# Order of every engine's work written by a list schedule at build time, in an attention and mixture-of-experts layer

## The chip, the cores and the metric

One core of one Trainium2 chip runs the whole kernel. The metric is the device time in microseconds of one execution. Below, PE is TensorE, DVE is VectorE, ACT is ScalarE, POOL is GpSimd and SP is the engine that issues the plain transfers.

## The reference

Eight sequences of 512 rows of 128 numbers go through one layer.

```
q, k, v = x @ Wq, x @ Wk, x @ Wv             # 16 heads of 8 numbers; q and k are rotated (rope)
attn = softmax(causal(q @ k.T / sqrt(8)))    # 512 x 512 per head
x1 = layernorm(x + (attn @ v) @ Wo)
shared = (silu(x1 @ sw1) * (x1 @ sw3)) @ sw2                 # every row, width 256
logits = x1 @ router_w.T + experts_bias; two best of 8 experts, softmax over the two
moe = sum over the two of weight * (silu(x1 @ w1[e]) * (x1 @ w3[e])) @ w2[e]
out = layernorm(x1 + moe + shared)
```

## The kernel before

The work is cut into small parts, each with a kind and a key. Sequence s is in the keys; so `values.2.1` is the part `values` of sequence 2 with its second group of four heads. For each sequence PE does `x_T` (x is transposed), `project` twice (q and k with their rotated copies), `v`, then bursts. A `burst` is the unit of the scores: it makes scores of one block of heads for the row maxima, which DVE takes from them (`max`), and, for the block three blocks earlier (`LEAD = 3`), the scores again with the maxima in them, of which ACT takes the exponential (`scores` on ACT) and on which POOL zeroes what the causal mask hides (`scores` on POOL). Four blocks of five bursts make a sequence, 40 units of scores. The maxima go through PE (`max_rows`), DVE and an SP transfer (`maxima`) into the stack of q and k that the second scores read; q and k themselves are split in three bf16 parts (`rope`, `rest`, `low`, on POOL and ACT, for the first sequence on DVE), stored (`store_parts`) and loaded back (`stack`). `values` multiplies the masked exponentials by v, for ten units each; `heads_T`, `out_T`, `out`, then on DVE `ln1_stats` and `ln1` (with a power on POOL between them) give x1. PE transposes it (`x1_T`) and computes the router's logits (`router`).

The expert part is made of steps: a shared step per 128 rows, and routed tiles of 128 rows sorted by expert. Groups of sequences are sorted together: `SORTED = [[0, 1], [2, 3], [4, 5], [6], [7]]`, which makes 23 tiles for a pair and 15 for one. For a group PE counts (`count`, `rank`), POOL writes the rows of x1 to their places in memory (`scatter`, eight per sequence), SP loads them in fours (`load_rows`) and loads the weights of each tile (`weight`, a ring of four). Per step: `T` (rows transposed), `gate` on PE, `tanh` on ACT, `glu` on DVE, `down` on PE. Results are stored (`store_rows`), gathered by POOL (`gather`), and finished by DVE (`combine`, `ln2_stats`, `ln2`).

Every engine runs its own fixed list and waits at semaphores when what it needs isn't there. What sets the lists is one table. A time in units of scores stands for each kind in `AT`; `LATER` moves a kind on one engine; each engine's list is all events sorted by that time:

```
        return [(kind, key) for _, _, kind, key in
                sorted((at + LATER.get((engine, kind), 0), n, kind, key) for at, n, kind, key in events if kind != "step")]
```

PSUM is shared by order too: the small results of PE take two banks in turn (`RING`), the projections, maxima scores and heads take two others in turn (`m_use`), so an engine's place in the list also decides which bank it waits for. Lines that the steps below touch: L665 `x_T`, L673 `project`, L679 `v`, L686 the scores of a burst, L719 `max_rows`, L732 `values`, L744 `heads_T`, L766 `x1_T`, L773 `router`, L826 `gate`, L838 `down`, all on PE; L903 `max`, L945 `ln1` and `ln2` on DVE, L1029 and L1037 `glu`; L548 the exponentials and L561 `rope` on ACT; L484 the masks, L496 `scatter`, L506 `gather`, L332 `rope` on POOL; L361 `store_parts`, L374 `stack`, L380 `maxima` on SP.

Of the kernel before, what the change touches and what calls it, by code (L numbers as in the profile page):

```python
# [27 lines left out]
SORTED = [[0, 1], [2, 3], [4, 5], [6], [7]]  # L28

AT = dict(values=2.39, v=9.96, rows1=12.08, maxima1=11.92, heads_T0=3.87, heads_T1=5.09, out_T=6.97, out=8.09,
          ln1_stats=8.24, ln1=9.29, x1_T=10.6, router=10.9, weights=11.33, load_residual=-9.49, load_x=-66.56,
          x_T=-58.7, project0=-56.05, project1=-57.45, rope=-52.94, rest=-50.5, low=-45.97, store_parts=-42.99,
          stack0=-39.65, stack1=-15.2, rows0=-8.24, maxima0=-8.23, count=12.23, rank=12.56, scatter=14.13,
          scatter_step=0.52, shared=11.71, shared_step=2.7, routed=28.08, margin=1.02, apart=1.0, T=-1.89, tanh=-0.0,
          glu=0.16, down=1.98, stored=4.65, weight_late=1.33, gather=6.58, gather_step=1.39, combine=1.9,
          lull_from=-4.81, lull_to=17.29, lull=1.0, routed_last_but_one=-0.14, routed_last=0.07, apart_last=1.0,
          gather_last=7.56, gather_step_last=1.43, combine_last=7.65)


LATER = {("act", "T"): 0.17, ("act", "ln1"): -0.41, ("act", "ln2"): 0.14, ("act", "out"): -0.33, ("act", "rest"): 2.75,
         ("act", "rope"): 2.16, ("act", "weights"): 0.16, ("act", "x_T"): -0.18, ("dve", "count"): -0.5,
         ("dve", "max"): 0.18, ("dve", "max_rows"): -0.5, ("dve", "rank"): 0.28, ("dve", "router"): -0.5,
         ("pool", "ln2"): -0.33, ("pool", "low"): -0.5, ("pool", "product"): 1.64, ("pool", "rest"): 0.55,
         ("pool", "rope"): -0.5, ("pool", "scores"): 0.76, ("pool", "shared_rows"): 0.44}


def build_block(nc, x, wq, wk, wqr, wkr, wv, wo, cos, sin, ident, mask, router, bias, experts, consts, out):
    B, S, D = x.shape  # L50
# [5 lines left out]
    T = S // P  # L56
# [115 lines left out]
    STEP = [key for _, key in steps]  # L172
    step_of = {key: i for i, key in enumerate(STEP)}

    def line(engine):
# [5 lines left out]
    RING = ("x_T", "v", "values", "max_rows", "out_T", "out", "x1_T", "router", "count", "rank", "T", "down")  # L181
# [31 lines left out]
    with ExitStack() as ctx:  # L213
# [437 lines left out]
        def _(pe):  # L651
# [37 lines left out]
            def burst(n, b):  # L689

                scored = n - LEAD
                if scored >= 0:
                    s, block = scored // BLOCKS, scored % BLOCKS
                    half = scored // 2
                    first = NU * 2 * scored + 2 * b
                    if scored % 2 == 0 and b == 0:
                        pe.wait_ge(max_in, (half + 1) * 48)
                    for pair in range(2):
                        if first + pair >= 2:
                            pe.wait_ge(exp_done, first + pair - 1)  # L700
                        for at_piece, (k, j, at) in enumerate(PAIR_UNITS[b]):
# [450 lines left out]
```

## Time and profile before

| | us |
|---|---|
| median of three runs | 780.66 (780.32 to 781.21) |
| the profiled execution, its own time | 776.18 |
| span in the profile | 774.1 |
| PE busy | 600.5 (78%) |
| DVE busy | 475.7 (61%) |
| ACT busy | 323.9 (42%) |
| POOL busy | 322.0 (42%) |

Busy time is the sum of an engine's instructions. The span less the busy time is what an engine waited, for other engines, for transfers, or for nothing that the profile can name ("issue"). The mean clock granted to PE over the span was 0.864 of full speed.

### The profile page before, as it was taken

How to read it: one execution, taken by the hardware profiler on the slowest of the kernel's cores; microseconds unless marked ns; L12 is line 12 of the kernel's file. 1: busy time of each engine (PE TensorE's matmuls, PEld its weight loads, DVE VectorE, ACT ScalarE, POOL GpSimd, SP SyncE). 2: the span in 40 equal slices, each digit the busy share in tenths (PEclk: the TensorE clock that was granted, in tenths of full speed). 3: DMA queues.
4: the chain of work that ended last, by engine and by line, in shares of the span. 5: the costliest groups of instructions: out<-in, count | busy, mean ns of one | idle time of the engine just before them, and what ended most of it. 6: DMA issues, size and time to landing. Idle time of an engine off the chain costs nothing.

```text
span 774.1 us, 14746 instructions
## 1 busy us (share of the span) xinstructions
PE 600.5 (78%) x4363; PEld 381.2 (49%) x4363; DVE 475.7 (61%) x1957; ACT 323.9 (42%) x771; POOL 322.0 (42%) x530
## 2 busy tenths in 40 slices
PE   3378988887878889888887998887898887786650
PEld 1123224424534565466544754655566665586640
DVE  3477747675537777776568877765578731644342
ACT  2016543563226455643364447524464455213320
POOL 4033431262275223424686326218447445442313
PEclk9567868978679999999899899979799999868985
DMA  3742220220224634622455345413575375435741
GB/s 92 214 143 87 63 91 2 76 83 8 70 89 141 185 93 130 180 93 86 153 163 149 94 151 157 127 47 122 159 217 169 93 210 165 133 102 158 203 111 54
DMA packets 80062, 94.08 MB, mean 122 GB/s; under 512 B 10224, under 2 KB 61168, under 8 KB 79984
## 3 DMA queue, kind: packets, MB, share of 16 engines
q1 hardware_dynamic: 75888, 84.75, 37.3%
q0 software_dynamic: 4096, 8.40, 3.4%
q8 instruction: 36, 0.59, 0.3%
q14 instruction: 42, 0.34, 0.1%
HBM read 70.37 MB, written 22.35 MB: 120 GB/s over the span
## 4 chain that ended last, share of the span: by engine, by line
PE 51%; issue 15%; DVE 15%; POOL 8%; ACT 6%; DMA 3%; SPq 1%; another core or an unknown queue 0%; POOLq 0%; ACTq 0%; DVEq 0%
PE ps L826 12%; PE ps L732 11%; PE ps L686 9%; PE ps L838 7%; PE ps L673 4%; POOL yg L506 3%; DVE sums L903 3%; ACT probs L548 3%; DVE gate L1029 2%; POOL rows_in L496 1%; PE ps L773 1%; DVE acc L1046 1%; PE ps L744 1%; POOL qk L332 1%; ACT th L607 1%
## 5 line engine op out<-in xcount | busy, mean ns | idle before, releaser
L903 DVE CUSTOM_DVE_ANT_0 sums<-ps,mask_sb 128x384 bf16<-128x384 f32 (+3 forms) x512 | 222.0, 486 | 51.9 <-PE ps L686 43.1
L484 POOL TENSOR_SCALAR_AFFINE_SELECT probs<-probs 128x256 f32<-128x256 f32 (+1 forms) x320 | 114.7, 364 | 263.7 <-ACT probs L548 260.6
L686 PE MATMUL ps<-stack 64*128 64x128 bf16 (+3 forms) x1024 | 160.2, 334 | 61.1 <-ACT probs L548 20.1
L548 ACT ACTIVATE probs<-ps 128x512 f32<-128x512 f32 x320 | 183.5, 597 | 44.2 <-PE ps L686 41.6
L1029 DVE SCALAR_TENSOR_TENSOR gate<-th,ps 128x256 f32<-128x256 f32 x131 | 54.8, 418 | 122.3 <-ACT th L607 104.2
L826 PE MATMUL ps<-xgT,w_tile 128*128 128x128 f32 x792 | 119.7, 299 | 12.0 <-issue 6.8
L686 PEld LDWEIGHTS ps<-stack 64*128 64x128 bf16 x1024 | 48.9, 97 | 144.0 <-DVE negmax L903 38.8
L826 PEld LDWEIGHTS ps<-xgT,w_tile 128*128 128x128 f32 x792 | 106.4, 209 | 21.9 <-issue 15.2
L607 ACT ACTIVATE th<-ps 128x256 f32<-128x256 f32 x131 | 50.3, 384 | 110.5 <-PE ps L826 89.6
L732 PE MATMUL ps<-probs,va 128*32 128x512 f32 (+3 forms) x1024 | 90.9, 503 | 6.8 <-POOL probs L484 2.8
L838 PE MATMUL ps<-w_tile,hid 128*128 128x128 f32 x396 | 70.6, 305 | 24.7 <-DVE hid L1037 13.1
L506 POOL DMA_INDIRECT yg<-rows_out,slot x64 | 61.4, 959 | 44.3 <-DVE acc L1046 19.6
L496 POOL DMA_INDIRECT rows_in<-x,slot x64 | 62.8, 982 | 32.1 <-DVE slot L1021 17.4
L838 PEld LDWEIGHTS ps<-w_tile,hid 128*128 128x128 f32 x396 | 57.5, 209 | 36.6 <-DVE hid L1037 19.2
L732 PEld LDWEIGHTS ps<-probs,va 128*32 128x32 f32 x1024 | 34.1, 123 | 65.0 <-issue 53.7
L580 ACT ACTIVATE ot<-ps 128x512 f32<-128x512 f32 x32 | 19.1, 597 | 91.1 <-PE ps L732 81.8
L620 ACT ACTIVATE y_routed<-ps 128x128 f32<-128x128 f32 x99 | 27.6, 278 | 47.5 <-PE ps L838 36.1
L1037 DVE TENSOR_TENSOR hid<-gate,ps 128x256 f32<-128x256 f32 x99 | 41.6, 421 | 3.4
L903 DVE DVE_READ_ACCUMULATOR2_ANT negmax<- 128x1 f32 x512 | 42.3, 83 | 0.0
L826 PE MATMUL ps<-x1T,w_shared 128*128 128x128 f32 x256 | 41.6, 314 | 0.0
L826 PEld LDWEIGHTS ps<-x1T,w_shared 128*128 128x128 f32 x256 | 37.3, 224 | 1.7 <-issue 1.0
L601 ACT ACTIVATE xgT<-ps 128x128 f32<-128x128 f32 x99 | 27.6, 279 | 12.9 <-PE ps L809 9.7
(105 smaller groups left out, 605.0 us busy)
## 6 DMA issues: line engine op xcount, KB each, us to landing
w_tile<-in_experts SPq DMA_DIRECT2D x99, 384.0 KB
stack<-parts_scratch SPq DMA_DIRECT2D x112, 128.0 KB
rows_out<-y_routed SPq DMA_DIRECT2D x99, 64.0 KB
parts_scratch<-parts SPq DMA_DIRECT2D x16, 384.0 KB
xg<-rows_in SPq DMA_DIRECT2D x21, 256.0 KB
rows_in<-zeros SPq DMA_DIRECT2D x2, 1472.0 KB, 10.5
x_t<-in_x SPq DMA_DIRECT2D x8, 256.0 KB, 2.9
x_r<-in_x SPq DMA_DIRECT2D x8, 256.0 KB
```

Source lines behind the costliest of these rows:

```text
L484: pool.affine_select(out=area, in_=area, compare_op=ALU.is_ge, fill=0.0, base=0, pattern=pattern, channel_multiplier=-1).then_inc(masked, 1)
L496: pool.indirect_dma_start(out=rows_in[g % 2], out_offset=bass.IndirectOffsetOnAxis(ap=slot[:, r, s, t:t + 1], axis=0), in_=x1[:, s % X1RIN ...
L506: pool.indirect_dma_start(out=yg[:, t, r, :], out_offset=None, in_=rows_out[g % 2], in_offset=bass.IndirectOffsetOnAxis(ap=slot[:, r, s, t ...
L548: act.activation(probs[:, (s * NB + v) % PRING, :], ps[:, SC + v % 2, :], ACT.Exp, scale=SCALE).then_inc(exp_done, 1)
L607: act.activation(th[:, i % 2, :], ps[:, GU + i % 2, 0:2 * P], ACT.Tanh, scale=0.5).then_inc(th_done, 1)
L686: return pe.matmul(ps[:, bank, at:at + width], here[:, stationary, at_s:at_s + P], here[:, moving, at_m:at_m + width], start=True, stop=True)
L732: last = pe.matmul(ps[32 * k:32 * k + 32, bank("values", s, g), j * P:S], va[:, j, PER_PV * g + k, :], probs[:, (s * NB + v) % PRING, at:a ...
L826: last = pe.matmul(ps[:, GU + i % 2, j * P:(j + 1) * P], w[:, j * P:(j + 1) * P], moving, start=True, stop=True)
L838: last = pe.matmul(ps[:, bank("down", i), 0:D], hid[:, i % HRING, half * P:(half + 1) * P], w[:, (4 + half) * P:(5 + half) * P], start=(ha ...
L903: ins = dve.tensor_tensor_reduce(sums[:, use % 2, at:at + w], ps[:, M + use % 2, at:at + w], mask_sb[:, S - w:S], -1.0, 3.0e38, ALU.add, A ...
L1029: link(dve.scalar_tensor_tensor(out=gate[:, i % 2, :], in0=th[:, i % 2, :], scalar=1.0, in1=bank[:, 0:2 * P], op0=ALU.add, op1=ALU.mult), ...
L1037: dve.tensor_tensor(hid[:, i % HRING, :], gate[:, i % 2, :], bank[:, 2 * P:4 * P], ALU.mult).then_inc(hid_done, 1)
```

## The change

All of `AT` and `LATER` have new numbers, and the list of an engine is no longer the sorted table. `COST` gives each part on each engine two numbers of nanoseconds: how long it takes the engine, and how long until what it made can be used. `needs` names for each part those whose end it waits for: data, buffers of each ring, and engines behind them. `plan` then walks through time at build: whenever an engine is free, it takes, among the kinds whose next part has all its needs met, the one with the lowest number of the table, so a part that isn't ready by the estimate lets others pass it. Within a kind the order stays that of the table. Which of the two ring banks is free is followed too. Rings, tile shapes, bursts and transfers are as they were, and so is every wait of the kernel; the instructions that each part issues are the same.

```diff
-AT = dict(values=2.39, v=9.96, rows1=12.08, maxima1=11.92, heads_T0=3.87, heads_T1=5.09, out_T=6.97, out=8.09,
+AT = dict(values=3.65, v=8.47, rows1=13.37, maxima1=40.13, heads_T0=4.31, heads_T1=4.33, out_T=1.93, out=9.25,
...
+COST = dict(
+    pe=dict(x_T=(480, 700), project=(1850, 2100), v=(950, 1200), max_rows=(120, 350), values=(2500, 2700), heads_T=(950, 1200),
+            out_T=(480, 700), out=(950, 1200), x1_T=(480, 700), router=(950, 1200), count=(600, 850), rank=(1800, 2050),
+            T=(120, 350), gate=(970, 1200), down=(490, 700), burst=(900, 1150)),
...
+    pool=dict(rope=(2150, 2200), rest=(2150, 2200), low=(2150, 2200), scores=(400, 460), scatter=(980, 3000),
+              gather=(980, 3200), shared_rows=(440, 500), ln1=(1030, 1090), ln2=(1030, 1090)),
...
+            if kind == "x1_T":
+                return [("dve", "ln1", s, 0)] + [("pe", "gate", step_of[("shared", s - 2, t)]) for t in range(T) if s >= 2]
...
+            if kind == "values":
+                found = [("pool", "scores", s, UPG * key[1] + UPG - 1)]
+                return found + [("act", "v", s, 0), ("pe", "heads_T", s - 1, 1)] if key[1] == 0 else found
...
+            best = None
+            for kind, found in queue[engine].items():
+                if not found:
+                    continue
+                part = found[-1]
+                if waits[part] or due[part] > now or best is not None and parts[best] <= parts[part]:
+                    continue
+                if engine == "pe":
+                    if kind in RING and len(ring) >= 2 and ends.get(ring[-2], now + 1) > now:
+                        continue
+                    if kind in ("project", "burst", "heads_T") and banks and ends.get(banks[-1], now + 1) > now:
+                        continue
+                elif engine == "dve" and kind in ("project", "max", "heads_T") and banks[drained] != part:
+                    continue
+                best = part
...
+            lines[engine].append((kind, key))
+            taken, lasts = COST[engine][kind]
...
+            free[engine] = now + taken
+            ends[best] = now + lasts
...
+            for part in then.get(best, ()):
+                waits[part] -= 1
+                due[part] = max(due[part], now + lasts)
+                if not waits[part]:
+                    tries.append((max(due[part], free[part[0]]), part[0]))
...
     def line(engine):
-
-        return [(kind, key) for _, _, kind, key in
-                sorted((at + LATER.get((engine, kind), 0), n, kind, key) for at, n, kind, key in events if kind != "step")]
...
+        return lines[engine]
```

The program grew by 270 lines above the engines' code, so L766 of before is L1036 of the changed kernel, and so with the others. Three places show how the lists move.

**The end of the first sequence's attention, on PE.** Before, from its `out` (L758) on: `v` of the next sequence, the last burst of a block, then `x1_T` and `router` in a row.

```order
161 L751 MATMUL ps<-ident_sb,on 128x128 x4
162 L686 MATMUL ps<-stack 128x256 x8
163 L758 MATMUL ps<-wo_sb,onT 128x128 x4
164 L679 MATMUL ps<-wv_sb,xT 128x128 x4
165 L686 MATMUL ps<-stack 128x512 x4
166 L766 MATMUL ps<-ident_sb,x 128x128 x4
167 L773 MATMUL ps<-router_sb,x1T 128x8 x4
168 L826 MATMUL ps<-x1T,w_shared 128x128 x4
```

The same place of the changed kernel, from `out` (L1028) to `x1_T` (L1036) and what follows it.

```order
164 L1028 MATMUL ps<-wo_sb,onT 128x128 x4
165 L956 MATMUL ps<-stack 128x256 x8
166 L956 MATMUL ps<-stack 128x512 x4
167 L1002 MATMUL ps<-probs,va 32x512 x4
168 L1002 MATMUL ps<-probs,va 32x384 x4
169 L1002 MATMUL ps<-probs,va 32x256 x4
170 L1002 MATMUL ps<-probs,va 32x128 x4
171 L956 MATMUL ps<-stack 128x512 x4
172 L1036 MATMUL ps<-ident_sb,x 128x128 x4
173 L989 MATMUL ps<-ident_sb,negmax 32x128
174 L956 MATMUL ps<-stack 128x384
```

`v` now stands ahead of `heads_T`, three bursts and one `values` stand between `out` and `x1_T`, and a burst (rows 174 to 181) stands between `x1_T` and `router`, which is row 182. In the expert steps, too, a `down` mostly comes one part later after its `gate` than before.

**The start, on PE.** Before, after the first `x_T`: both projections of sequence 0, then bursts, with `x_T` and both projections of sequence 1 among the bursts further on.

```order
1 L665 MATMUL ps<-ident_sb,x_t 128x128 x4
2 L673 MATMUL ps<-xT,wk_sb 128x512
3 L673 MATMUL ps<-xT,wkr_sb 128x512
4 L673 MATMUL ps<-xT,wq_sb 128x512
5 L673 MATMUL ps<-xT,wqr_sb 128x512
6 L686 MATMUL ps<-stack 128x512 x4
```

In the changed kernel `v` of sequence 0, `x_T` of sequences 1 and 2 and the projections of sequence 1 stand ahead of the first burst.

```order
1 L935 MATMUL ps<-ident_sb,x_t 128x128 x4
2 L943 MATMUL ps<-xT,wk_sb 128x512
3 L943 MATMUL ps<-xT,wkr_sb 128x512
4 L949 MATMUL ps<-wv_sb,xT 128x128 x4
5 L935 MATMUL ps<-ident_sb,x_t 128x128 x4
6 L943 MATMUL ps<-xT,wq_sb 128x512
7 L943 MATMUL ps<-xT,wqr_sb 128x512
8 L935 MATMUL ps<-ident_sb,x_t 128x128 x4
9 L943 MATMUL ps<-xT,wk_sb 128x512
10 L943 MATMUL ps<-xT,wkr_sb 128x512
11 L943 MATMUL ps<-xT,wq_sb 128x512
13 L956 MATMUL ps<-stack 128x512 x4
```

The second projection of sequence 0 (rows 6 and 7) comes behind `v` and an `x_T`. On ACT the copies of `v` and of both `x_T` likewise stand ahead of the first `rope`; and on SP the `store_parts` and `stack` of sequence 1 come ahead of the first `maxima`, where before the first `maxima` came ahead of them.

**The scatters of the first group, on POOL.** Before, the sixteen scatters (L496) alternate with the masks (L484) that PE's `values` wait for.

```order
57 L484 AFFINE_SELECT probs<-probs 128x128 x4
58 L496 DMA rows_in<-x,slot 2944x128 x2
59 L484 AFFINE_SELECT probs<-probs 128x2x128
60 L496 DMA rows_in<-x,slot 2944x128 x2
61 L484 AFFINE_SELECT probs<-probs 128x2x128
62 L496 DMA rows_in<-x,slot 2944x128 x2
```

In the changed kernel twelve scatters (L766) stand in a row, and after them three and one.

```order
56 L754 AFFINE_SELECT probs<-probs 128x2x128 x6
57 L785 TENSOR_TENSOR acc<-x,y_shared 128x128
58 L754 AFFINE_SELECT probs<-probs 128x128
59 L766 DMA rows_in<-x,slot 2944x128 x12
60 L754 AFFINE_SELECT probs<-probs 128x128
61 L766 DMA rows_in<-x,slot 2944x128 x3
62 L754 AFFINE_SELECT probs<-probs 128x128
63 L766 DMA rows_in<-x,slot 2944x128
66 L602 TENSOR_TENSOR qk<-qk,rest 128x1024
```

The masks of the second group of heads of sequence 2 are now all ahead of the scatters, and nine of the ten masks of its third group, with the `rope` of sequence 4 (L602) among them, behind twelve or more. The next two groups have runs of ten scatters in the same way.

## Rows read from the trace of the kernel before

**Rows 1.** The page, busy time and share of each engine.

```profile
PE 600.5 (78%) x4363; PEld 381.2 (49%) x4363; DVE 475.7 (61%) x1957; ACT 323.9 (42%) x771; POOL 322.0 (42%) x530
```

**Rows 2.** Windows: stretch, its length, busy us of PE, PEld, DVE, ACT, POOL, clock, DMA.

```profile
113.00:178.00 65.00, 53.58 (x366) 25.54 (x366) 43.98 (x191) 30.56 (x60) 23.26 (x48) 0.84 0.17 50
178.00:264.00 86.00, 67.86 (x487) 40.04 (x488) 51.51 (x224) 35.82 (x78) 40.21 (x67) 0.84 0.34 103
```

**Rows 3.** Waits of PE over the span: total us, times, longest.

```profile
PE ps L686 <- ACT probs L548: 20.1, 34, 2.5
...
PE ps L838 <- issue: 13.9, 7, 5.1
PE ps L838 <- DVE hid L1037: 13.1, 17, 2.0
PE ps L766 <- DVE x L945: 12.8, 8, 2.8
PE ps L686 <- DVE negmax L903: 10.4, 35, 1.1
...
PE ps L732 <- POOL probs L484: 2.8, 1, 2.8
PE ps L773 <- ACT x1T L590: 2.7, 4, 0.7
```

**Rows 4.** Timeline of PE, sequence 0's x1_T: start, us, instruction, idle before.

```profile
125.47 1.01 PE L766 MATMUL ps<-ident_sb,x 128*128 128x128 f32 x4 [2.54 <-DVE x L945]
127.16 1.88 PE L773 MATMUL ps<-router_sb,x1T 128*128 128x8 f32 x8 [0.69 <-ACT x1T L590]
128.89 2.05 PE L826 MATMUL ps<-x1T,w_shared 128*128 128x128 f32 x8
...
136.92 1.16 PE L826 MATMUL ps<-x1T,w_shared 128*128 128x128 f32 x8
```

**Rows 5.** Timeline of the start, to the first `v`; PE and SP (SPq).

```profile
18.80 0.90 SPq L361 DMA_DIRECT2D parts_scratch<-parts  x2
22.51 4.45 SPq L374 DMA_DIRECT2D stack<-parts_scratch  x7
...
29.33 0.61 PE L686 MATMUL ps<-stack 64*128 64x512 bf16 x2 [17.24 <-DMA stack<-parts_scratch]
...
33.66 5.73 SPq L456 DMA_DIRECT2D rows_in<-zeros  x2
...
37.89 1.12 PE L665 MATMUL ps<-ident_sb,x_t 128*128 128x128 f32 x4
...
45.23 1.02 PE L673 MATMUL ps<-xT,wqr_sb 128*128 128x512 f32 x2
...
53.42 1.76 SPq L380 DMA_DIRECT2D stack<-mparts  x3
...
65.47 2.07 PE L679 MATMUL ps<-wv_sb,xT 128*128 128x128 f32 x8
```

**Rows 6.** Timeline of PE (a burst, a values) and of POOL at the scatters.

```profile
104.39 1.29 PE L686 MATMUL ps<-stack 64*128 64x256 bf16 x5 [0.18 <-DVE negmax L903]
...
107.81 4.49 PE L732 MATMUL ps<-probs,va 128*32 128x512 f32 x32
...
147.09 2.36 PE L732 MATMUL ps<-probs,va 128*32 128x512 f32 x32
...
221.59 0.96 POOL L496 DMA_INDIRECT rows_in<-x,slot  x1 [0.30 <-issue]
...
222.98 0.41 POOL L484 TENSOR_SCALAR_AFFINE_SELECT probs<-probs 128x256 f32<-128x256 f32 x1
...
234.65 2.35 POOL L332 TENSOR_TENSOR qk<-qk,rest 128x1024 f32<-128x1024 f32 x1
```

**Rows 7.** Timeline of the tail: last result of PE copied, first gather of the last sequence.

```profile
749.59 0.28 ACT L620 ACTIVATE y_routed<-ps 128x128 f32<-128x128 f32 x1 [1.10 <-PE ps L838]
...
753.86 1.01 POOL L506 DMA_INDIRECT yg<-rows_out,slot  x1 [0.19 <-issue]
```

More of the change, by code:

```diff
@@ L42 @@
[L42 to L46, printed above, removed]
+AT = dict(values=3.65, v=8.47, rows1=13.37, maxima1=40.13, heads_T0=4.31, heads_T1=4.33, out_T=1.93, out=9.25,
+          ln1_stats=3.38, ln1=-9.96, x1_T=13.1, router=12.46, weights=13.68, load_residual=-22.41, load_x=-41.11,
+          x_T=-59.34, project0=-55.44, project1=-56.69, rope=-51.57, rest=-52.7, low=-46.79, store_parts=-45.6,
+          stack0=-35.09, stack1=-22.24, rows0=-9.01, maxima0=20.63, count=13.49, rank=22.77, scatter=15.95,
+          scatter_step=0.42, shared=13.66, shared_step=2.82, routed=31.73, margin=1.16, apart=1.05, T=-3.21,
+          tanh=-18.58, glu=2.43, down=4.48, stored=7.03, weight_late=-1.27, gather=6.2, gather_step=1.42,
+          combine=3.37, lull_from=16.73, lull_to=10.1, lull=0.33, routed_last_but_one=9.41, routed_last=-7.45,
+          apart_last=2.4, gather_last=-10.13, gather_step_last=0.03, combine_last=7.34)
@@ new lines @@
+LATER = {("act", "down"): -0.88, ("act", "out"): 4.9, ("act", "rest"): 5.58, ("act", "rope"): -5.98, ("act", "scores"):
+         0.49, ("act", "tanh"): 9.0, ("act", "v"): 2.61, ("act", "values"): -2.48, ("act", "weights"): -10.6,
+         ("act", "x1_T"): 4.06, ("act", "x_T"): 9.03, ("dve", "combine"): -4.26, ("dve", "count"): 0.89,
+         ("dve", "heads_T"): 4.27, ("dve", "ln1"): 10.23, ("dve", "ln1_stats"): -6.76, ("dve", "ln2"): 11.66,
+         ("dve", "ln2_stats"): 0.38, ("dve", "low"): -7.04, ("dve", "max"): -0.79, ("dve", "max_rows"): 0.62,
+         ("dve", "project"): 23.4, ("dve", "rank"): -8.33, ("dve", "rest"): -4.08, ("dve", "rope"): 13.76,
+         ("dve", "router"): 31.87, ("dve", "weights"): 0.58, ("pe", "T"): 1.69, ("pe", "burst"): -1.28, ("pe",
[3 rows of a table added]
+         1.37, ("pool", "gather"): -1.22, ("pool", "ln1"): -3.24, ("pool", "ln2"): -2.62, ("pool", "low"):
+         3.93, ("pool", "rest"): 3.28, ("pool", "rope"): -4.9, ("pool", "scores"): -0.11, ("pool",
+         "shared_rows"): -0.1, ("sp", "load_residual"): -0.87, ("sp", "load_rows"): -16.88, ("sp", "load_x"):
+         2.91, ("sp", "maxima"): -5.14, ("sp", "out_rows"): 25.54, ("sp", "stack"): -12.96, ("sp",
+         "store_parts"): 12.55, ("sp", "store_rows"): 7.18, ("sp", "weight"): 4.53}
@@ L173, in build_block @@
     step_of = {key: i for i, key in enumerate(STEP)}
+    RING = {"x_T": "act", "v": "act", "values": "act", "max_rows": "dve", "out_T": "act", "out": "dve", "x1_T": "act",
+            "router": "dve", "count": "dve", "rank": "dve", "T": "act", "down": "act"}
+    READER = {"out_T": "out", "out": "ln1_stats"}
+    order_of = {}
+    for at, _, kind, key in sorted(events, key=lambda event: event[:2]):
+        order_of.setdefault(kind, []).append((at, key))
+    placed = {(kind, *key): at for at, _, kind, key in events}
@@ L175, in line @@
+    lines, planned = plan()
+    PLANNED.append(planned)
     def line(engine):
-        return [(kind, key) for _, _, kind, key in
-                sorted((at + LATER.get((engine, kind), 0), n, kind, key) for at, n, kind, key in events if kind != "step")]
-    RING = ("x_T", "v", "values", "max_rows", "out_T", "out", "x1_T", "router", "count", "rank", "T", "down")
+        return lines[engine]
     ring_use, m_use, weight_use, rows_use, routed_use, shared_use = {}, {}, {}, {}, {}, {}
```

215 lines of the change are left out of this document (207 added, 8 removed), and 3 rows, old and new, of the table LATER.

## The prediction

> **What bounds the kernel now.** I read the busy shares first [rows 1]: PE is busy 600.5 of 774.1 us and DVE 475.7; ACT and POOL are at 42%. PE is the engine with most work, and 173.6 us of its span are waits. Next come the windows by sequence [rows 2]. In the stretch 113 to 178, which holds one sequence and no routed tiles, PE is busy 53.6 of 65.0 us and DVE 44.0; in 178 to 264, where the first group is scattered, PE is busy 67.9 of 86.0 and DVE 51.5. So PE leads in both, DVE follows at two thirds, and in the second stretch POOL alone goes up, from 23 to 40 us. PE's waits [rows 3] are many and short. The longest wait in any of those groups is 5.1 us and most are under 1 us. They say that PE stands in its list before something that another engine has in hand, while other parts for PE would be ready. That is what an order can mend. About 22 us are outside it: PE's first burst starts at 29.33 after a wait of 17.24 us for a transfer [rows 5], with only some 7 us of PE work before, and the end, from 749.6 on, has no PE work at all [rows 7].
>
> **The start.** Before, PE waits to 29.33, and then does sequence 1's `x_T` and projections among the bursts, from 37.89 to 46.25 with 1.5 us of burst matmuls between them: 6.9 us that now stand in the empty time. `v` (2.07 us at 65.47) and one more `x_T` (1.12) move there as well [rows 5]. Together 10.1 us. Against it, sequence 0's second projection now stands behind `v` and an `x_T`, some 2 to 3 us, and ACT copies the third `x_T`, for which a load of x has to come in between, before the first `rope`. I put that `rope` 2.5 to 3.8 us later, so `store_parts` (18.80) and the first burst (29.33) as well, and take 3. That would leave 7 us gained. But the second scores need the first `maxima`, issued at 53.42, and on SP these now stand behind sequence 1's `store_parts` and `stack`, all of it issued in order. I count it out: `store_parts` at 21.8; its stack 3.7 later (22.51 after 18.80) at 25.5; two stacks of 4.45 to 34.4; 5.73 us for the zeros and some 1.5 for three small loads to 41.7; the next `store_parts` and its stack the same 3.7 and 4.45, to 49.9, or 50.4 with the seam between them. So the first `maxima` leave 3 us earlier than before, and the first scores gain 3 and not the 4 that were left of 6.9. With `v` and the other `x_T`, 3.2 in all, the total of the start is **6 us** gained (bounds: 2 if the `rope` is later still, 8).
>
> **The wait before x1_T.** Each sequence ends in a chain on DVE, POOL and DVE of some 4 us, for which PE had `v` and one burst, and stood 1.3 to 2.8 us before `x1_T`: 12.8 us in eight waits [rows 3], 2.54 of them in [rows 4]. Now three bursts and one `values` stand between. A burst goes at 1.29 + 0.18 = 1.47 us, a `values` at 2.36 [rows 6]: 6.8 us of work against 4, so I take all 12.8. `router` likewise waited for ACT's copy (2.7 us in four waits [rows 3]) and has a burst before it now: 2.7. After the stop the clock was low: the first `gate` took 2.05 us where a later one took 1.16 [rows 4], and `router` 1.88. I count 0.9 us for each of these two in the two or three sequences where it shows, of 5.4 at most: 3.5.
>
> [...]
>
> **The steps.** PE waited 13.1 us before `down` for `hid`, in 17 waits, and 13.9 us for "issue" [rows 3]. With a burst or another `gate` in between, the first is mostly gone; of the second I don't know what it is (a weight tile that isn't there would look so) and take nothing, with 13.9 as the upper bound. I take 10 of the 13.1. The waits of bursts for exponentials and maxima (20.1 and 10.4 [rows 3]) are waits for ACT's and DVE's own pace; I take nothing there, and half of them, 15, as the bound.
>
> **What is given back.** 12.8 + 2.7 + 3.5 + 10 = 29 us of waits disappear from PE. Not all of it comes out of the time: with PE faster, DVE, at 44 of 65 us [rows 2], is asked for `max` and `glu` sooner and banks come free later than PE wants them. I take a third off, as an estimate between nothing and everything: **19 us** gained (bounds 5 and 29).
>
> **The scatters.** This is what speaks against the change. POOL needs 0.96 + 0.30 = 1.26 us for each scatter in a row, the table of costs says 0.98; so twelve take 15.1 us and not 11.8, in which no mask is done. In the first group POOL has, from the time the slots are known to the last mask of the third `values` of sequence 2: 16 scatters, 20.2 us; nine masks of 0.41 with 0.17 between them, 5.2; one `rope`, 2.35; three small adds, 1.4: 29 us [rows 6], and I take the slots to come 2 us after `rank`, which is the price of DVE's part, an estimate. PE has from `rank` to that `values`: four `down` of about 0.6 (half a gate), two gates of 1.16, seven bursts of 1.47, four passes of projection of 1.02, one `values` of 2.36 and small ones, 22.5 us. So it stands some 8.5 us. Before, the same stage had one wait of 2.8 us for POOL [rows 3], at the second `values`, which is gone. Net 5.7; I take **5 us** lost (0 if more of PE's list fits in, up to 9 more in each of the two next groups, where PE has four more gates and downs to cover it). What is queued behind the run on POOL are masks, `rope` and with it the next `store_parts`; PE's `values` waits for the masks, and after such a stop it may run at 4.49 us instead of 2.36 [rows 6].
>
> **The tail.** The gathers of the last sequence were issued behind `ln2` of sequence 6, from 753.86, 4.3 us after PE's last result was copied at 749.59 [rows 7]; a store has to land in between, for which I take 2.7 us as an estimate, the kernel's own table having 2.5; so 1.6 us are to be had, since sequence 6 is now combined some eight tiles earlier. Its three parts of DVE work then stand among the last gates, whose cover is only one `down` and one transpose; I count 1.6 us lost there. Sum nothing; bounds 2 either way.
>
> **Sum.** 6 + 19 − 5 = 20 us. Against the profiled execution's 776.2 this is 756; the median of the runs is 4.5 us over it, so 780.7 − 20 = **760.7**.
>
> **The rivals.**
> Fast: nothing is given back and half the waits for exponentials and maxima go as well. 6 + 29 + 15 − 5 = 45 us, 736 (728 to 748). For it: every wait is short and PE work was ready; the clock at 0.84 [rows 2] has room. Against: DVE's share.
> Moved waits: only the start and a sixth of the 29 us are gained, because a denser PE meets DVE and ACT at once. 6 + 5 − 5 = 6 us, 775 (770 to 780). For it: 34 and 35 waits for ACT and DVE [rows 3] show how close these follow.
> Slower: the run of scatters holds PE in all three large groups. Each costs 8.5 us and 2.1 us for one `values` at the low clock, 32 us less the 2.8; if also nothing but 10 of the 29 us comes, 6 + 10 − 29 = −13, or 794; with all 19, 785. I put it at 783 to 795. It decides when POOL's waits pass 25 us in total. Against it: from the second group on, PE has routed steps to do meanwhile, so its cover there is 27 us and more against POOL's 31. That the new order does nothing at all can't be: the lists differ all through.
>
> **Chances.** My forecast (748 to 770) 0.43, fast 0.20, moved waits 0.20, slower 0.17. The range 736 to 786 leaves out a tenth on either side. What a measurement of this kernel tells from no change is about 0.2%, 1.6 us. Faster: 0.43 + 0.20 and most of the moved waits, 0.79; same 0.04; slower 0.17.
>
> **What would show it.** In the changed profile the waits for L945 before `x1_T` should be gone or under 3 us, those for `hid` under 5; the first burst should start near 32 and the first scores near 54; `values` of sequence 2 should wait several us for POOL masks in the first group; PE busy should be a little under 600. I am wrong on the slow side if waits for masks sum to over 25 us, or if SP, whose list now has `maxima` behind the next `store_parts`, holds bursts up; wrong on the fast side if the granted clock of the stretches with sequences is well above 0.84 and PE busy falls by more than 10 us.

## The result: slower in the first measurement, faster in two later ones on other chips

On the chip of the first measurement the changed kernel took **793.29 us** (median of 4, 791.05 to 795.57), the kernel before 780.93 (780.32 to 782.74): ratio 1.0155, 95% interval 1.0121 to 1.0188, slower by 12.4 us. The forecast was 760.7. The same two kernels, unaltered, ran in two more sets later, on chips 2 and 13 (the record gives no number for the first chip): 741.63 against 767.08 (ratio 0.9665, 0.9618 to 0.9713) and 744.51 against 766.56 (0.9694, 0.9655 to 0.9733), a gain of 25.5 and 22.1 us. Ratios here and below leave out executions in the chip's slower state, so that a ratio need not be the quotient of the two medians beside it. Both results are far outside the noise; the experiments say what parts them. In the rows, L956 is the scores of a burst, L1002 `values` and L1108 `down`.

The page of the changed kernel, first chip, answers to [rows 1]:

```profile
PE 609.9 (77%) x4363; PEld 383.4 (48%) x4363; DVE 479.0 (61%) x1957; ACT 324.8 (41%) x771; POOL 322.9 (41%) x530
```

The windows of the same run answer to [rows 2]:

```profile
113.00:178.00 65.00, 53.43 (x379) 26.41 (x379) 45.33 (x195) 31.00 (x62) 24.45 (x50) 0.84 0.16 50
178.00:264.00 86.00, 63.73 (x455) 36.36 (x454) 49.57 (x212) 33.35 (x72) 38.98 (x64) 0.78 0.28 86
```

The first stretch is as it was, with 13 more matmuls in it (379 for 366). The second, with the first group's scatters, has 455 matmuls where [rows 2] has 487, and its granted clock fell from 0.84 to 0.78. The waits of PE, answering to [rows 3]:

```profile
PE ps L956 <- DVE negmax L1173: 23.4, 51, 1.5
PE ps L1002 <- issue: 14.3, 17, 1.7
PE ps L956 <- DVE qk L1163: 10.7, 1, 10.7
PE ps L956 <- ACT probs L818: 9.9, 15, 2.3
PE ps L1002 <- POOL probs L754: 6.8, 5, 2.7
PE ps L1108 <- DVE hid L1307: 6.4, 8, 2.1
...
PE ps L1043 <- ACT x1T L860: 0.9, 2, 0.6
```

The 12.8 us before `x1_T` are gone, `x1T` went from 2.7 to 0.9 and `hid` from 13.1 to 6.4 (with 4.9 us of waits for `hid` before gates, which are new). So most of the gains came. Two lines are new: 14.3 us of "issue" inside `values`, and one wait of 10.7 us for DVE. The timelines of PE, POOL, ACT and DVE around it show what it is:

```profile
211.57 2.36 PE L1002 MATMUL ps<-probs,va 128*32 128x512 f32 x32
213.86 1.12 PE L943 MATMUL ps<-xT,wk_sb 128*128 128x512 f32 x2
...
216.22 0.40 PE L956 MATMUL ps<-stack 64*128 64x384 bf16 x4
227.33 1.25 PE L956 MATMUL ps<-stack 64*128 64x384 bf16 x4 [10.71 <-DVE qk L1163]
```

```profile
208.60 1.19 POOL L766 DMA_INDIRECT rows_in<-x,slot  x1 [0.51 <-issue]
...
222.75 0.96 POOL L766 DMA_INDIRECT rows_in<-x,slot  x1 [0.31 <-issue]
```

```profile
224.39 0.60 ACT L850 ACTIVATE ot<-ps 128x512 f32<-128x512 f32 x1 [11.84 <-remote]
```

```profile
226.58 0.69 DVE L1163 TENSOR_TENSOR qk<-ps,cos_sb 128x512 f32<-128x512 f32 x1 [12.93 <-remote]
```

PE's `values` was over at 213.93 and its first projection at 214.98. ACT, which copies the one, starts at 224.39; DVE, which reads the other, at 226.58. Neither had anything else to do, and neither waits in the program for one of the scatters (the only wait for POOL in it, DVE's for `low` of the sequence before, had been met at 162.4). "remote" in the rows means that what ended the wait can't be told from the profile. POOL's twelve scatters run from 208.60 to 223.71. On a later chip the same stretch of the same kernel reads so, POOL's rows being the same within 0.1 us:

```profile
213.98 1.12 PE L943 MATMUL ps<-xT,wk_sb 128*128 128x512 f32 x2
...
216.34 0.80 PE L956 MATMUL ps<-stack 64*128 64x384 bf16 x8
217.91 1.10 PE L943 MATMUL ps<-xT,wq_sb 128*128 128x512 f32 x2 [0.77 <-DVE negmax L1173]
...
230.90 1.03 PE L956 MATMUL ps<-stack 64*128 64x512 bf16 x3 [7.53 <-ACT probs L818]
```

```profile
222.83 0.96 POOL L766 DMA_INDIRECT rows_in<-x,slot  x1 [0.31 <-issue]
```

```profile
214.15 0.60 ACT L850 ACTIVATE ot<-ps 128x512 f32<-128x512 f32 x1 [1.49 <-PE ps L1002]
```

```profile
215.22 0.69 DVE L1163 TENSOR_TENSOR qk<-ps,cos_sb 128x512 f32<-128x512 f32 x1 [1.44 <-PE ps L943]
```

Here ACT and DVE start 0.1 us after PE is done. In the second large group of the first chip it hits `values` itself: its matmuls come one at a time, and the profile finds nothing that they wait for ("issue").

```profile
372.09 2.02 PE L1002 MATMUL ps<-probs,va 128*32 128x512 f32 x17
375.15 0.42 PE L1002 MATMUL ps<-probs,va 128*32 128x256 f32 x2 [1.04 <-issue]
375.89 0.38 PE L1002 MATMUL ps<-probs,va 128*32 128x256 f32 x1 [0.32 <-issue]
377.99 1.31 PE L1002 MATMUL ps<-probs,va 128*32 128x256 f32 x2 [1.73 <-issue]
```

It ends at 386.57, after 14.5 us; on the later chip:

```profile
363.22 2.36 PE L1002 MATMUL ps<-probs,va 128*32 128x512 f32 x32
```

**Late signals.** A signal is the raise of a semaphore, by which one engine tells another that its work is done. The traces record when each one is raised. For every matmul of PE that raises one, I took the time from its end to the next raise of that semaphore, and sorted by how many of GpSimd's indirect transfers had ended in the 6 us before. The share over 1 us late, changed kernel (number of matmuls in brackets; a few raises are missing from a trace, which adds some false ones):

```
transfers in 6 us     0          1         2         3         4         5
first chip        0.00 (928) 0.15 (48) 0.43 (58) 0.42 (55) 0.47 (62) 0.95 (20)
a later chip      0.00 (829) 0.02 (56) 0.00 (48) 0.05 (82) 0.00 (95) 0.00 (61)
```

Below, "late" for a run is the sum over stretches in which PE raised nothing and the first raise due came over 2.5 us late: 12.3 us for the kernel before and 45.3 for the changed one on the first chip, 0.0 for both on the later one. The sum depends on how the edges of a stretch are drawn: a stricter and a looser count of the same traces give 37 and 53 for the changed kernel and 4 and 19 for the one before, while the zeros stay zeros. It shows where signals were late, and isn't a price in time: e7 below has 44.8 at 1.002 times the kernel before.

Not only PE's signals are late. The same count for the others, first chip, share over 1 us late with none, then with four transfers in 6 us: DVE 0.00 (754) and 0.33 (67), ACT 0.00 (581) and 0.46 (52), POOL's own 0.00 (329) and 0.19 (26).

### The profile page after: what moved, and what is told of

It reads as the page before. It is cut to its first block, busy times and chain, and to the rows that moved or that the text cites. A ratio compares the mean times of both kernels' runs of the same rounds, so it can differ in the third digit from the quotient of the medians.

```text
span 791.5 us, 14747 instructions
## 1 busy us (share of the span) xinstructions
PE 609.9 (77%) x4363; PEld 383.4 (48%) x4363; DVE 479.0 (61%) x1957; ACT 324.8 (41%) x771; POOL 322.9 (41%) x530
## 4 chain that ended last, share of the span: by engine, by line
PE 44%; DVE 17%; issue 12%; POOL 9%; DMA 6%; another core or an unknown queue 5%; SPq 5%; ACT 3%; POOLq 0%; DVEq 0%; ACTq 0%
PE ps L1002 11%; PE ps L1096 10%; PE ps L956 7%; PE ps L1108 6%; DVE sums L1173 5%; POOL yg L776 5%; PE ps L943 3%; DMA rows_out<-y_routed 2%; SPq L644 2%; PE ps L1014 2%; DMA yg<-rows_out,slot 1%; DVE acc L1316 1%; POOL probs L754 1%; DVE gate L1299 1%
## 5 line engine op out<-in xcount | busy, mean ns | idle before, releaser
L818 ACT ACTIVATE probs<-ps 128x512 f32<-128x512 f32 x320 | 176.6, 598 | 64.9 <-PE ps L956 60.6
L956 PE MATMUL ps<-stack 64*128 64x512 bf16 (+3 forms) x1024 | 156.2, 332 | 59.2 <-DVE negmax L1173 23.4
L1096 PE MATMUL ps<-xgT,w_tile 128*128 128x128 f32 x792 | 121.4, 302 | 9.4 <-issue 5.8
L1002 PE MATMUL ps<-probs,va 128*32 128x512 f32 (+3 forms) x1024 | 107.1, 527 | 23.5 <-issue 14.3
L956 PEld LDWEIGHTS ps<-stack 64*128 64x128 bf16 x1024 | 46.2, 97 | 144.6 <-DVE negmax L1173 47.6
L1108 PE MATMUL ps<-w_tile,hid 128*128 128x128 f32 x396 | 68.3, 299 | 24.6 <-DVE hid L1307 6.4
L1002 PEld LDWEIGHTS ps<-probs,va 128*32 128x32 f32 x1024 | 37.6, 126 | 92.9 <-issue 74.6
L766 POOL DMA_INDIRECT rows_in<-x,slot x64 | 62.4, 974 | 30.3 <-issue 17.9
L1108 PEld LDWEIGHTS ps<-w_tile,hid 128*128 128x128 f32 x396 | 55.8, 204 | 34.3 <-issue 21.1
L785 POOL TENSOR_TENSOR acc<-x,y_shared 128x128 f32<-128x128 f32 x32 | 14.6, 457 | 48.8 <-ACT y_shared L885 48.7
## 6 DMA issues: line engine op xcount, KB each, us to landing
rows_in<-zeros SPq DMA_DIRECT2D x2, 1472.0 KB, 10.2
```

Of the source, the lines that this page charges most:

```text
L766: pool.indirect_dma_start(out=rows_in[g % 2], out_offset=bass.IndirectOffsetOnAxis(ap=slot[:, r, s, t:t + 1], axis=0), in_=x1[:, s % X1RIN ...
L818: act.activation(probs[:, (s * NB + v) % PRING, :], ps[:, SC + v % 2, :], ACT.Exp, scale=SCALE).then_inc(exp_done, 1)
L956: return pe.matmul(ps[:, bank, at:at + width], here[:, stationary, at_s:at_s + P], here[:, moving, at_m:at_m + width], start=True, stop=True)
L1002: last = pe.matmul(ps[32 * k:32 * k + 32, bank("values", s, g), j * P:S], va[:, j, PER_PV * g + k, :], probs[:, (s * NB + v) % PRING, at:a ...
L1096: last = pe.matmul(ps[:, GU + i % 2, j * P:(j + 1) * P], w[:, j * P:(j + 1) * P], moving, start=True, stop=True)
L1108: last = pe.matmul(ps[:, bank("down", i), 0:D], hid[:, i % HRING, half * P:(half + 1) * P], w[:, (4 + half) * P:(5 + half) * P], start=(ha ...
```

## Experiments

Eighteen more runs were made, in five sets, each set on one chip beside the kernel before, whose median was 780.4 (e1 to e4), 778.1 (e5 to e8), 770.4 (e9 to e12), 767.1 (r1 to r4) and 766.6 (s1, s2). Times of different sets are compared by their ratio to it. In the expectations of e1 to e6 theory A is that the transfers hold up the other engines, and B that GpSimd's occupancy and late masks do (my rival "Slower"); in e1 and e3 there is also C, neither.

**e1_pairs.** GpSimd's list with at most two scatters in a row:

```diff
+    def apart(parts, kinds, most):
+        out, held = [], []
+        for part in parts:
+            if part[0] in kinds:
+                held.append(part)
+                continue
+            out += held[:most]
+            held = held[most:]
+            out.append(part)
+        return out + held
+    lines["pool"] = apart(lines["pool"], ("scatter",), 2)
```

> The changed kernel with one thing altered: GpSimd's list has at most two scatters in a row, the others held back until a mask (or other part of the list) has passed; the order of the scatters among themselves and of all the rest is kept, and so are the four other engines' lists. Theory A (a long run of indirect transfers on GpSimd holds up the issue and the semaphores of all the other engines, whatever they wait for): the stalls at values 2.2, 4.1 and 6.1 (14.5 and 16.7 us for the last two, where one usually takes 2.4) and at the two later runs of 7 and 8 go, which is 25 to 38 us: 755 to 770 us. Theory B (GpSimd's occupancy and late masks, my rival Slower: the work of GpSimd is the same and only its order is other): the masks come earlier but the scatters later, and later row loads hold the experts; 780 to 795 us. Theory C (the lower clock and the other engines' lists are what costs, not GpSimd): 790 to 796 us.

780.42 us, ratio 1.0029 (0.9988 to 1.0069): some 10 us better than the changed kernel, not the 25 to 38 of theory A, and at the lower edge of B's range. Late 40.1 us, so the signals were as late with pairs as with runs; DVE's timeline has

```profile
382.65 0.56 DVE L1186 CUSTOM_DVE_ANT_0 sums<-ps,mask_sb 128x384 bf16<-128x384 f32 x1 [8.50 <-remote]
```

A mask of 0.3 us between pairs hardly thins them out: 14 scatters in 18.1 us, 1.4 each.

**e2_pause.** The lists untouched; ahead of each scatter

```diff
+                    pool.memset(pause[:, paused:paused + 1], 0.0)
```

> The changed kernel, lists untouched, with a memset of one column on GpSimd ahead of each scatter (96 more instructions on GpSimd, about 0.1 us each). It parts theory A from B most sharply, since it makes GpSimd's runs longer and not shorter. Theory A, in the form that it is the unbroken row of indirect transfers that holds the others up: 755 to 772 us. Theory A in the form that it is the number of transfers in a stretch of time, broken or not: no change, 790 to 797. Theory B (masks late behind GpSimd's work): 0 to 5 us slower than the changed kernel, 793 to 798.

796.05 us, ratio 1.0232 (1.0132 to 1.0332), late 50.1 us. That is no gain, within B's range and within that of A's second form. The memset took 0.11 us and fitted into the 0.3 us between two scatters, so it altered neither pace nor length. A row without anything between its transfers is not what matters, and e2 doesn't part A from B.

**e3_before_runs.** The kernel before, its 16 scatters of each large group in one run:

```diff
+            for g in (0, 1, 2):
+                own = [part for part in found if part[0] == "scatter" and part[1][0] == g]
+                at = found.index(own[6])
+                found = [part for part in found[:at] if part not in own] + own + [part for part in found[at:] if part not in own]
```

> The kernel before with one thing altered: in each of the three large groups the 16 scatters stand in one run on GpSimd, at the place of the seventh, where they stood in ones and twos between the masks; nothing else moves. Theory A: PE, VectorE and ScalarE stall together from about 5 us after a run's start until its end, 3 times 12 to 16 us: 815 to 830 us. Theory B: the masks behind a run come up to 10 x 1.26 = 12.6 us later, of which the distance between mask and use covers a part: 785 to 805 us, and only what reads a mask waits. Theory C: within 3 us of the kernel before.

810.62 us, ratio 1.0396 (1.0283 to 1.051), 30.2 us slower: between A's and B's ranges, nearer to A. The windows of its three runs of scatters, from some 5 us after their start, columns as in [rows 2]:

```profile
216.00:231.00 15.00, 2.47 (x8) 0.90 (x8) 2.86 (x9) 1.19 (x2) 11.64 (x14) 0.57 0.20 73
378.00:392.00 14.00, 2.63 (x22) 1.85 (x20) 1.30 (x3) 1.15 (x3) 10.65 (x12) 0.76 0.44 145
554.00:569.00 15.00, 4.35 (x30) 3.34 (x29) 0.84 (x2) 1.61 (x5) 11.34 (x13) 0.68 0.45 144
```

PE, DVE and ACT together do almost nothing, 9.5, 5.0 and 4.0 us in 44. Part of that may be masks that were missing.

**e4_before_pause.** The kernel before with e2's memset ahead of each scatter and gather.

> The kernel before with a memset of one column on GpSimd ahead of each scatter and each gather, lists untouched. Theory A: the short stalls that it already has (about 5 us around its run of 7 scatters, 3 us in its run of gathers) go: 772 to 778 us. Theory B: no gain, 780 to 784 us.

786.97 us, ratio 1.0091 (1.0036 to 1.0146), late 21.5 us. No gain, and 3 us above B's range too: a miss for A in the form in which I had it.

**e5_no_scatter.** Each scatter becomes a memset of the same length that signals in its place:

```diff
-                pool.indirect_dma_start(
-                    out=rows_in[g % 2], out_offset=bass.IndirectOffsetOnAxis(ap=slot[:, r, s, t:t + 1], axis=0),
-                    in_=x1[:, s % X1RING, t, :], in_offset=None).then_inc(scattered[g % 2], 16)
+                pool.memset(pause[:, :], 0.0).then_inc(scattered[g % 2], 16)
```

> The changed kernel, all lists untouched, with each of the 64 scatters replaced by a memset of 128x1340 on GpSimd, about 1.2 us, that signals in its place (the rows are then never moved: the routed experts work on zeros, and the output lacks their part). GpSimd is as long busy as before, so its masks come as late as in the changed kernel, but no indirect write is made. What it leaves out is the 64 transfers. Theory A (the transfers themselves hold up the other engines' completions): 755 to 770 us, and the values of the large groups take 2.4 us again instead of 14 and 16. Theory B (GpSimd's occupancy and late masks): 786 to 795 us. Since the signals of PE in e1 and in the changed kernel came up to 10 us after its matmuls were issued, in stretches with a scatter every 1.3 us, I expect A.

744.07 us, ratio 0.956 (0.9467 to 0.9654), late 0.0. Its first run of memsets is as long as that of scatters,

```profile
208.55 15.88 POOL L771 MEMSET pause<- 128x1340 f32 x12
```

twelve in 15.88 us, 1.32 each, where the scatters took 15.1. The first mask behind it starts at 224.38 (223.73 in the changed kernel), and 49 us are gone, or 47 against e8 below, which has the same lists and all its scatters and ran on the same chip. This settles B: the masks come as late as in the changed kernel, and it costs nothing like that. Nor was this chip free of the effect: beside the gathers, which e5 keeps, 0.28 (61) and 0.32 (57) of PE's signals came over 1 us late with three and with four of them in 6 us, in stretches too short to count in the sum. The memsets also spare the wait for the rows to land and the rows are zeros; e6 has both of these too, and gains only 2 us by it.

**e6_before_no_scatter.** The same edit of the kernel before.

> The kernel before with the same replacement: each of its 64 scatters is a memset of 128x1340 on GpSimd that signals in its place (the rows are never moved, so the output lacks the routed experts' part). Its scatters stood in pairs between masks. Theory A: it loses only the few short hold-ups that its trace shows (8 us at 220 to 228, 4 us at 692 to 697, some of it hidden), 768 to 778 us. Theory B: within 3 us of the kernel before, 778 to 784. The difference between this and e5 is what the new order is worth without transfers: 15 to 22 us gained under A, by my forecast's own terms; none or a loss under B.

775.82 us, ratio 0.9977 (0.9937 to 1.0018): the kernel before loses at most 5 us to its scatters, and e5 is 32 us below it. So without the transfers of the scatters the new order was worth 4.1%, on the same chip, above the 20 us that I forecast.

**e7_singles.** As e1 with `most` 1, in the three large groups.

> As e1, with at most one scatter between two masks (or other parts) of GpSimd's list in the three large groups. Theory A by the density of transfers: the distance from one scatter to the next goes from 1.4 us on the mean to 1.7 or more, and the late signals shrink: 765 to 778 us. But the last scatter, and with it the group's row load on which PE waited 8.6 us once in e1, comes later: if that weighs more, 780 to 790 us. A broken run would then not be the cure.

782.11 us, ratio 1.002 (0.9969 to 1.0071), late 44.8. Thinner by list alone trades one wait for another; the row that PE's transposes wait for:

```profile
PE ps L1092 <- DMA xg<-rows_in: 37.8, 3, 19.1
```

**e8_traffic.** Eight more loads of 64 KB on SP's queue beside each large group's scatters:

```diff
+                    for _ in range(8):
+                        loaded += 1
+                        sp.dma_start(unused[:, :], ident).then_inc(unused_in, 16)
+                        sp.wait_ge(unused_in, 16 * loaded)
```

> The changed kernel with 8 more loads of 64 KB on SP's queue in each large group, one after another's landing (about 2 us each), beginning when the scatters begin; the tile that they fill is read by nobody. In the traces the late signals of PE fall in stretches in which GpSimd scatters and SP's queue moves nothing (0.00 MB in the 4 us windows at 216, 220, 364 and 368), while in the kernel before equally dense scatters beside 0.2 to 0.9 MB of loads show none. If the quiet queue is part of the cause, and not its consequence, 768 to 782 us; if it is a consequence, or chance, no gain: 791 to 800 us.

790.89 us, ratio 1.0135 (1.0048 to 1.0221), late 32.7. That is no gain clear of noise against the changed kernel's 1.0155. The quiet queue was a consequence, or chance.

**e9_plain_writes, e10_half, e11_no_transfers, e12_replanned** ran on another chip. The edits: each scatter a plain DMA to fixed rows; e5's memset for every second scatter; e5 with the gathers replaced as well; and two numbers of the planner:

```diff
-scatter_step=0.42
+scatter_step=0.8
-scatter=(980, 3000)
+scatter=(1270, 3000)
```

> The changed kernel, lists untouched, with each scatter made a plain DMA of the same 64 KB from GpSimd's queue, to consecutive rows (so the rows go to the wrong experts' places). It asks whether the indirection or GpSimd's way of making a transfer is what costs. With all scatters taken out the same lists ran in 744.07 us, with them in 793.29. If any transfer that GpSimd issues so densely holds up the others: 780 to 800 us. If only the indirect ones, or if the plain one is issued in much less time: 742 to 760 us.

> The changed kernel with every second scatter (the second choice of each token) replaced by a memset of 128x1340 on GpSimd of the same length, so that half of the rows never move. GpSimd's occupancy stays; transfers come at 2.5 us instead of 1.26. If the cost is so much for each transfer, half of the 49 us between the changed kernel and e5 goes: 766 to 771 us. If it is their density that costs (late signals in 0.4 to 1.0 of the cases at 4 or 5 transfers in the last 6 us, and in 0.1 to 0.4 at 1 or 2), more than half goes: 746 to 762 us. If occupancy were the cost: 790 or more.

> As e5, with the 64 gathers replaced too (a memset of their length, then one of the tile that they would fill; the output lacks the routed experts' part, as in e5). e5's trace has late signals only in stretches with gathers, some 6 us in two large ones. 732 to 742 us if gathers hold up the others as scatters do; within 2 us of e5, 742 to 746, if not.

> The changed kernel with two numbers of its planner altered: a scatter is due 0.8 after the one before instead of 0.42, and occupies GpSimd for 1270 ns in the plan instead of 980. The plan then has 5 to 9 scatters in a row and the rest one to a mask, and gives the other engines' parts their places with that in view. If the late signals follow the runs, 775 to 785 us; the rows of a group come later, as in e7, and that may cost as much as it saves: 785 to 795 us. Nothing in it should reach e5's 744.

724.41 (ratio 0.943), 738.79 (0.9614), 730.72 (0.9436) and 734.89 us (0.9578, 0.9525 to 0.9631). All four came out below their ranges, e12 by 40 us, which said something was wrong with the comparison and not only with the kernel: e9, e10 and e12 have 0.0 late, e12's gathers in runs of up to eight included, and the kernel before was itself 8 to 10 us faster than in the sets before. (The expectation of e11 takes 5.9 us of late signals for e5's; they were e6's.)

**r1 to r4.** So the changed kernel, the kernel before, e12 and e10 ran once more, unaltered, together.

> The changed kernel, unaltered, once more. If the scatters' density costs on every chip: 785 to 797 us, 1.2 to 1.9% above the kernel before, with late signals in its three runs of 10 to 12 scatters. If the late signals are a matter of the chip: on a chip without them 738 to 750 us, 3 to 5% below the kernel before, and none of its signals late.

> The kernel before, unaltered, for its profile on this chip: a ratio of 1.00 with itself. On a chip with late signals about 780 us, with the two stretches of them (4 and 8 us); on one without, 763 to 772 us and none.

> e12 once more, beside the changed kernel on the same chip. If its pace of scatters (5 to 7 in a row, then one to a mask) is the cure: 733 to 740 us, 6 to 7% below the changed kernel. If the chip was it: within 1% of the changed kernel where no signals are late, and 775 to 790 us where they are.

> e10 once more (every second scatter a memset of the same length; half of the rows never move). If its 738.8 us came from halving the transfers: again 735 to 745 us beside a changed kernel at 790. If from the chip: within 1% of the changed kernel where no signals are late, 755 to 770 us where they are.

741.63 us for the changed kernel (0.9665), 767.28 for the one before (1.0003, 0.9972 to 1.0034), 735.79 for e12 (0.9589, 0.9544 to 0.9633) and 741.29 for e10 (0.9649, 0.9587 to 0.9712). No late signal in any of the four. Where signals come in time, halving the transfers is worth nothing (741.29 against 741.63): no cost of a scatter beyond GpSimd's 1.26 us shows in this pair. What e9 has over that is, as far as its trace goes, GpSimd's time (28 us less of it than in e12), though it wasn't tested by itself; the group of its 64 writes (busy time and mean ns, then idle time before them) is

```profile
L767 POOL DMA_DIRECT2D rows_in<-x x64 | 35.0, 556 | 12.5 <-DVE slot L1290 12.0 <-issue 0.5
```

556 ns for a plain transfer where an indirect one takes 960 and 300 more to the next.

**s1, s2.** e12 and the changed kernel on one more chip.

> e12 a third time. On a chip whose traces have no late signals: 733 to 740 us, 4% below the kernel before and 0.5 to 1% below the changed kernel. On one that has them: 770 to 788 us if the pace of scatters helps as little as in e1 and e7 (1.00 times the kernel before), 750 to 765 if it helps more.

> The changed kernel, unaltered, a third time, beside it on the same chip. 738 to 745 us where no signal is late; 788 to 796 us where they are.

737.92 us (0.9612, 0.9576 to 0.9648) and 744.51 (0.9694); late 0.0 in both. e12 is the best version that computes the reference: 0.8 and 0.9% below the changed kernel beside it, about 4% below the kernel before. It gains most plainly in the waits of bursts for exponentials, 21.2 us in r1 and 15.7 in r3, and there in the 7.53 us stop shown above. ACT's copy of a shared result waits there for POOL's add of the one before (8.18 us for `acc` in its timeline), and the add stands behind all sixteen scatters. In e12 it stands behind ten, and PE's stop at that place, in the trace of r3, is

```profile
226.04 1.52 PE L956 MATMUL ps<-stack 64*128 64x512 bf16 x4 [2.40 <-ACT probs L818]
```

Which of its two numbers does it wasn't tried. It never ran on a chip with late signals, so what it would do there stays open.

## Why the forecast failed on one chip and held on the others

**The step that failed** is "The scatters". It priced a scatter as 1.26 us of GpSimd's time and what is queued behind it there, 5 us lost. On the first chip it is also a delay of the signals of PE, DVE and ACT, which the forecast put at nothing: PE's late by 45.3 us in sum. Its price is some 47 to 52 us: e5 is 49 us below the changed kernel (46 by ratio: 1.0155 less 0.956, of 780) and 47 below e8, and the changed kernel itself took 52 and 49 us less where no signal was late (r1, s2). The kernel before took 14 us less there, of which its scatters had cost 2 to 5 (e6). So the new order gains 32 us (e5 against e6), and the delay takes that and 12 us more. These last figures can't check one another, since the changed kernel's own time is one of their terms. The kernel before had 12.3 us of late signals. Its scatters came at nearly the pace of e1's (ten in 13.2 us), and why e1's signals were late so much more isn't known.

**The rival "Slower"** gave 783 to 795 and the time fell into it, but by another mechanism. It wanted late masks in all three groups; the waits for masks sum to 6.8 us, not over 25, and e5 keeps the occupancy and loses the cost. A right number from a wrong cause.

Where signals are in time, the forecast held as a gain: 20 us, with 11 to 33 for its range. As a time it didn't, since the kernel before was 14 us faster there too, and 741.63 and 744.51 lie under the 748. The terms can be read one by one, r2 against r1, the waits of before first, then of the changed kernel:

```profile
PE ps L838 <- DVE hid L1037: 17.9, 20, 2.0
PE ps L686 <- DMA stack<-parts_scratch: 17.1, 1, 17.1
PE ps L686 <- ACT probs L548: 15.9, 32, 0.9
PE ps L766 <- DVE x L945: 14.2, 9, 2.8
PE ps L686 <- DVE negmax L903: 10.2, 35, 1.1
...
PE ps L838 <- DVE hid L1034: 7.5, 9, 1.7
```

```profile
PE ps L956 <- DVE negmax L1173: 24.1, 54, 1.6
PE ps L956 <- ACT probs L818: 21.2, 16, 7.5
PE ps L1108 <- DVE hid L1307: 9.1, 8, 4.4
PE ps L1002 <- POOL probs L754: 7.2, 8, 2.3
PE ps L956 <- DMA stack<-parts_scratch: 6.2, 1, 6.2
PE ps L935 <- DMA x_t<-in_x: 5.4, 2, 4.3
...
PE ps L956 <- DMA stack<-mparts: 4.6, 1, 4.6
PE ps L943 <- DVE qk L1163: 4.3, 1, 4.3
```

- **The start**, forecast 6 us gained: nothing. The first burst starts at 31.46, as forecast (32). The first scores start at 58.62 and not 54, after 4.6 us of waiting for the stacked maxima; before it was about the same time, and by 113 us the two kernels stand equal, with 362 matmuls done against 359. Of the 17.1 us at the start 6.2 are left, and 5.4, 4.6 and 4.3 of new waits (x, maxima, `qk`) take their place. SP's list in r1 shows what was mis-sized:

```profile
41.38 5.51 SPq L631 DMA_DIRECT2D parts_scratch<-parts  x2
50.53 5.06 SPq L644 DMA_DIRECT2D stack<-parts_scratch  x7
55.63 1.75 SPq L650 DMA_DIRECT2D stack<-mparts  x3
```

Up to `store_parts` of sequence 1 the count of the forecast is right: 41.38 against 41.7. But this store, behind the two fills with zeros, held SP for 5.51 us where the first one took 0.90, and its stack left 9.15 us after it and not 3.7. So the first `maxima` left at 55.63 and not at 50.4, later than before (53.77 in r2) and not earlier. Why the store took so long isn't shown.

- **The wait before x1_T**: 14.2 us are now under 1, as forecast. PE's busy time, in which the clock term of 3.5 us would show, fell by 3.9, from 591.8 to 587.9. At the first `x1_T` the `router` and the gate behind it take 1.88 and 2.05 us in r2, at a granted clock of 0.50 (127.80 to 131.60), and 1.03 and 1.14 us in r1, at 1.00 (131.30 to 133.40). Not all of that is gained: the `values` that r1 has ahead of them takes 3.72 us, at 0.63, the one that r2 has behind them 2.99.
- **The steps**: `hid` before `down` 25.4 us (17.9 + 7.5), now 9.5, with 3.4 of new ones before gates: 12.5 gained, forecast 10. The waits for `hid` before `down` stayed over the 5 us that I named as a sign.
- **What is given back**: forecast a third of 29 us, 10. It is there, and most plainly in one line: waits of bursts for DVE's `negmax` rose from 10.2 to 24.1, 13.9 us. That a denser PE ran into DVE's pace is my reading of it.
- **The scatters**: forecast one stop of 8.5 us in the first group and none later. Measured one of 7.53 and none later, though behind POOL's add and not behind its masks.
- **The tail**, forecast nothing, made of 1.6 us gained and 1.6 lost: from the copy of PE's last result to the first gather of the last sequence it is 2.64 us in r1 and 4.27 in r2, the 1.6 gained. The loss can't be told apart in the traces.
- **Sum**: forecast 20 us gained; 25.5 and 22.1 measured on these chips. It is close in part by luck: the start gave nothing, and some waits fell for which the forecast had no term, those for `xgT` from 15.7 to 4.2 us and those of bursts for `on` from 6.6 to 0.9.

## What to carry to other kernels

Before you trust a gain or a loss of a few per cent from a new order, run both kernels on more than one chip and at more than one time: here the sign changed between sets. When several engines stop at once while what they wait for is done, look at what else is running and not at the names in the wait; then replace the suspect by work of equal length on its own engine, which parts its occupancy from its side effects in one run. In a hand-made plan, keep a long run of one engine's transfers apart from short parts behind it that others wait for, and cost it at its measured pace (1.26 us, not 0.98).

## What was not expected of the hardware

On the first chip, signals of PE came over 1 us late in 15% of the cases with one indirect transfer of GpSimd's in the last 6 us, in 47% with four and in 95% with five, and without one in none (the changed kernel's trace); in e1 to e8 it was 30% to 50% with four. Signals of DVE and ACT were late too, in 33% and 46% of the cases with four, and even GpSimd's own, in 19%; gathers alone did it in e5, for PE in 28% of the cases with three and 32% with four. On the three later chips, in nine traces, no share of PE's is over 0.05, which missing raises may explain, at the same 0.96 + 0.30 us for each indirect scatter. Transfers on SP's queue alone did it nowhere in the changed kernel's trace: the column for none (0.00 of 928) holds all of SP's first 200 us, two fills of 1.47 MB among them. The three sets with late signals were also the first three in time, and no chip was measured twice for certain, so whether the chip or the time or something else decides it stays open, and so does what exactly holds the signals up. Whether plain writes (e9) or another pace (e12) avoid it is open too, since neither ran where signals were late.
